# Values on 64 rows, variance and logits side by side, token weights as a row, and the one-hot matrix as eight compares

## The reference

```python
# token selection
scores = einsum('bnd,d->bn', x, w) + b[0]
top_scores, top_indices = top_k(scores, 204)
h = take_along_axis(x, top_indices) * sigmoid(top_scores)[..., None]
# attention: q, k, v = layernorm(h) times Wq.T, Wk.T, Wv.T, plus biases
row_mask = (q[:, :, 0] != 0) & (k[:, :, 0] != 0)
prob = softmax(where(mask, q @ k.T / 8, -1e9)); prob = where(mask, prob, 0)
h = h + (prob @ v) @ Wo.T + bo
# mixture of 8 experts, two of them for a token
xn = layernorm(layernorm(h)) * gamma + beta
logits = xn @ Wr + br
w = softmax(top_k(logits, 2))           # spread over the 8 experts
y = sum over e of (gelu(xn @ W1[e] + b1[e]) @ W2[e] + b2[e]) * w[e]
out = h + y
```

## Time and profile before

| | |
|---|---|
| median of 3 runs | 241.83 us (241.67 to 241.98) |
| profiled execution | 241.94 us |
| its span | 240.1 us |
| mean granted TensorE clock | 0.994 |
| PE busy | 218.4 us, 91% |
| VectorE busy | 165.5 us, 69% |
| GpSimd busy | 149.9 us, 62% |
| ScalarE busy | 140.9 us, 59% |
| chain of waits, share of the span | PE 82%, VectorE 10%, ScalarE 3%, issue 2%, DMA 2% |
| DMA | 25.69 MB, mean 107 GB/s |

### The profile page before, as it was taken

The page is one execution under the profiler, slowest core; times in us unless marked ns, Lnnn a source line. Parts: engine busy times, 40 slices in busy tenths (PEclk is TensorE's granted clock), DMA queues, the critical chain, the costliest instruction groups (busy, mean ns, idle before and its releaser), DMA issues.

```text
span 240.1 us, 5180 instructions
## 1 busy us (share of the span) xinstructions
PE 218.4 (91%) x1612; PEld 122.8 (51%) x1612; DVE 165.5 (69%) x551; ACT 140.9 (59%) x343; POOL 149.9 (62%) x194
## 2 busy tenths in 40 slices
PE   0469699899999999999989999999999999999991
PEld 0345478576767676767534544354443534433420
DVE  3899998979899999765645463855657365483362
ACT  2333857767676767576675455555647556466530
POOL 4398584839895969541427784585755546556662
PEclk9999999999999999999999999999999999999997
DMA  5043831132413231102936706717576492854811
GB/s 147 4 135 116 152 119 53 52 117 77 131 43 122 59 100 40 35 28 61 230 86 152 163 0 158 160 26 179 122 183 145 115 239 65 190 111 120 185 29 35
DMA packets 18340, 25.69 MB, mean 107 GB/s; under 512 B 4746, under 2 KB 15370, under 8 KB 18314
## 3 DMA queue, kind: packets, MB, share of 16 engines
q10 hardware_dynamic: 6112, 13.50, 24.0%
q1 hardware_dynamic: 12138, 11.86, 18.7%
q0 software_dynamic: 64, 0.00, 0.0%
HBM read 23.40 MB, written 1.96 MB: 106 GB/s over the span
## 4 chain that ended last, share of the span: by engine, by line
PE 82%; DVE 10%; ACT 3%; issue 2%; DMA 2%; POOL 0%; ACTq 0%; DVEq 0%; POOLq 0%
PE PD L958 20%; PE PD L973 19%; PE PD L881 5%; PE PD L906 5%; PE PD L893 5%; PE PD L836 4%; PE PD L825 4%; PE PD L918 3%; DVE ahead L1139 3%; PE PD L870 3%; PE PD L923 3%; PE PD L860 2%; PE PD L934 2%; PE PD L983 2%; DMA tok_col<-in_L_tok_b 2%
## 5 line engine op out<-in xcount | busy, mean ns | idle before, releaser
L1280 DVE SCALAR_TENSOR_TENSOR ye<-PD,b_col,mb 128x408 f32<-128x408 f32 x64 | 41.0, 641 | 48.9 <-PE PD L973 48.0
L502 POOL TENSOR_TENSOR acc<-acc,ye 128x408 f32<-128x408 f32 x52 | 54.6, 1050 | 31.8 <-DVE ye L1280 29.1
L675 ACT ACTIVATE hid<-PD,b_eff 128x816 f32<-128x816 f32 x64 | 56.7, 935 | 26.1 <-PE PD L958 25.1
L958 PE MATMUL PD<-uT,w_g 64*128 64x408 f32 x256 | 53.0, 530 | 1.3 <-ACT hid L675 0.9
L973 PE MATMUL PD<-hid,w_sb 128*64 128x408 f32 x256 | 51.1, 519 | 0.2 <-DVE ye L1280 0.2
L634 ACT ACTIVATE E<-PD,nmax 102x204 f32<-102x204 f32 x64 | 26.7, 437 | 15.6 <-DVE nmax L1176 15.6
L958 PEld LDWEIGHTS PD<-uT,w_g 64*128 64x128 f32 x256 | 21.9, 186 | 20.3 <-ACT hid L675 6.7
L973 PEld LDWEIGHTS PD<-hid,w_sb 128*64 128x64 f32 x256 | 15.5, 136 | 32.0 <-issue 26.6
L479 POOL TENSOR_TENSOR rstd<-veps,neg_half 102x8 f32<-102x8 f32 x8 | 13.1, 1640 | 19.2 <-DVE veps L1198 19.2
L1139 DVE SCALAR_TENSOR_TENSOR ahead<-srow,score,PD 128x256 bf16<-128x256 f32 x56 | 23.0, 475 | 0.0
L1176 DVE TENSOR_REDUCE nmax<-PD 102x2 f32<-102x408 f32 x32 | 17.1, 575 | 2.5 <-PE PD L881 1.7
(11 more groups left out here) (169 smaller groups left out, 343.1 us busy)
## 6 DMA issues: line engine op xcount, KB each, us to landing
mb<-mixd ACTq DMA_DIRECT2D x28, 408.0 KB, 5.8
srow<-scored SPq DMA_DIRECT2D x7, 512.0 KB, 4.0
rdbc<-rdend SPq DMA_DIRECT2D x16, 102.0 KB, 2.8
rbc<-rstd2d SPq DMA_DIRECT2D x16, 102.0 KB, 2.9
mb<-mixd SPq DMA_DIRECT2D x4, 408.0 KB, 6.8
X<-in_x ACTq DMA_DIRECT2D x6, 256.0 KB, 3.1
out<-y SPq DMA_DIRECT2D x7, 204.0 KB
w_raw<-in_L_ffn_W SPq DMA_DIRECT2D x2, 256.0 KB, 5.6
```

The source lines that it names most:

```text
L502: pool.tensor_tensor(acc[n % 4][:, :], H[:, n, :] if e == 0 else acc[n % 4][:, :], ye[k % 4][:, :], ALU.add)\
L675: act.activation(hid[k % 4][:, :, :], hid_ps[k % 2][:, :, 0:C], ACT.Gelu, bias=b1_eff[:, e:e + 1]).then_inc(hid_ok, 1)
L958: last = pe.matmul(hid_ps[k % 2][:, p, 0:C], w1_g[halves[p], e, :], uT[halves[p], n, :], start=True, stop=True)
L1280: dve.scalar_tensor_tensor(out=ye[k % 4][:, :], in0=y_ps[k % 2], scalar=b2_col[:, e:e + 1], in1=mb[n % MB][:, e, :], op0=ALU.add, op1=ALU. ...
```

## The change

**Token weights.** `tok_row` is a row on one partition. SyncE loads the weight as its first DMA and ScalarE the bias as its second; GpSimd's two DMAs go. One matmul of one row of ones with that row (L1055) replaces the two transposes. It waits for the DMAs and for VectorE's first memsets, no longer for GpSimd's constants.

**Gate.** `one_plus` (exp(-score) + 1, 128x8) moves from VectorE to ScalarE, right behind the exponential it uses at the start, and behind `copy_denT` in a stage.

**One-hot.** Eight `tensor_scalar` compares of 204 columns, each with a rank per partition from PSUM, replace the `tensor_tensor` of 1632. In stage 0, `copy_v(0)` and `row_max(0,0)` go ahead of `one_hot(1)`.

**Values.** Eight matmuls of 64 rows and 66 moving columns replace four of 128 rows and 132. v's layout follows, in SBUF and in PSUM.

**Variance** of units 0 to 5: `variance2_wide` is four matmuls with 32 weight columns (`ones2`, now 32 wide), each into 32 partitions of its own, behind `values`. ScalarE copies the tile and adds eps (`copy_wide2`). `variance2_rows` is one matmul between `attend(s-1,0)` and `scores(s,1)`, and ScalarE copies the 102x8 result behind `softmax(s,0)`; VectorE's `var_eps2` goes from the stages. Units 6 and 7, in the expert part, keep the old form.

**Logits** in the same way: four matmuls into 32 partitions each, a copy on ScalarE (`copy_logits`), and one transpose (`turn_logits`). The wide part of unit 0 lies ahead of `project(6)`, of unit 1 ahead of `project(7)`, and of unit n ahead of the `hidden` with k % 8 = 4; the transposes lie where `logits` was, but for unit 1, whose transpose moves to the end of stage 7.

**Mix.** One transpose of 102 x 64 in place of four; `copy_mT` is 64 x 102; `write_mix` writes 64 pieces of 408 bytes in place of 16 of 1632.

**Orders.** ScalarE's `copy_std2T(5)` and `gap_tanh(1)` go behind gelu(1). VectorE's `route(1,0)` goes ahead of `copy_ET0(7)`. The next to last store moves from SyncE to ScalarE.

The diff, cut to its core:

```diff
+            sp.dma_start(tok_row[:, 0:D], tok_w.unsqueeze(0)).then_inc(tok_in, 16)
             load_x0(sp, 0)
             load_x(sp, 1)
...
-                sp.dma_start(mixd[n], mT[:, :]).then_inc(mixd_ok, 16)
+                sp.dma_start(mixd[n].rearrange("r (g q) -> g r q", g=G), mT[:, :]).then_inc(mixd_ok, 16)
...
-            pool.dma_start(tok_col[:, 0:1], tok_w.unsqueeze(1)).then_inc(tok_in, 16)
-            pool.dma_start(tok_col[0:1, 1:2], tok_b.unsqueeze(1)).then_inc(tok_in, 16)
...
             load_x0(act, 1)
+            act.dma_start(tok_row[:, D:D + 1], tok_b.unsqueeze(0)).then_inc(tok_in, 16)
...
+            def one_plus_exp(u):
+                act.wait_ge(expneg_ok, u + 1)
+                if u == 0:
+                    act.wait_ge(dve_prep, 2)
+                if u >= 2:
+                    act.wait_ge(spread_ok, SPREAD * (u - 1))
+                    act.wait_ge(gate_ok, u - 1)
+                act.activation(one_plus[u % 2][:, :], expneg[:, :], ACT.Identity, bias=one_col[:, 0:1]).then_inc(plus_ok, 1)
...
+            def copy_wide2(u):
+                act.wait_ge(wide2p_ok, u + 1)
+                if u >= 1:
+                    act.wait_ge(var2p_ok, u)
+                act.activation(wide2[:, :], wide2_ps[u], ACT.Identity, bias=eps_col[:, 0:1]).then_inc(wide2_ok, 1)
+
+            def copy_var2(u):
+                act.wait_ge(var2p_ok, u + 1)
+                if u >= 1:
+                    act.wait_ge(rstd2_ok, u)
+                act.activation(veps2[:, :], var2_ps[u], ACT.Copy).then_inc(veps2_ok, 1)
...
+            def copy_logits(n):
+                if n >= 1:
+                    act.wait_ge(lgp_ok, n)
+                act.activation(lgw[:, :], lgw_ps[n], ACT.Copy).then_inc(lgw_ok, 1)
+
             def gelu(k):
                 e = k % NE
                 act.wait_ge(hidp_ok, k + 1)
+                if e == NE // 2 and k // NE + 2 < UNITS:
+                    copy_logits(k // NE + 2)
...
+                if s >= UNITS - 2:
+                    copy_logits(s - (UNITS - 2))
                 if (u := unit(s, 2)) is not None:
                     squares2(u)
+                    copy_wide2(u)
...
                 softmax(s, 0)
+                if (u := unit(s, 2)) is not None:
+                    copy_var2(u)
                 if (u := unit(s, 1)) is not None and s < UNITS - 1:
                     copy_OT(u)
                 softmax(s, 1)
...
             for k in range(K):
                 gelu(k)
-                if k == 0:
+                if k == 1:
                     copy_std2T(UNITS - 3)
                     gap_tanh(1)
-                if k == 1:
                     copy_denT(UNITS - 1)
                     copy_OT(UNITS - 1)
...
+                if u >= UNITS - 2:
+                    logits(u - (UNITS - 2))
...
-                        last = pe.matmul(v_ps[:, pr, qt * 2 * VX:(qt + 1) * 2 * VX], zT[u % 2][:, cols(pr, qt)],
-                                         wv_bd[:, :, :].rearrange("p a c -> p (a c)"), start=True, stop=True)
+                for i in range(2 * R):
+                    for p in range(2):
+                        last = pe.matmul(v_ps[:, p, i * VX:(i + 1) * VX], zT[u % 2][halves[p], i * Q:(i + 1) * Q],
+                                         wv_x[halves[p], :], start=True, stop=True)
...
+            def variance2_wide(u):
+                pe.wait_ge(sq2_ok, u + 1)
+                for g in range(G):
+                    last = pe.matmul(wide2_ps[u][32 * g:32 * (g + 1), :], ones2[:, :], sq2[:, g * Q:(g + 1) * Q],
+                                     start=True, stop=True)
+                last.then_inc(wide2p_ok, 1)
+
+            def variance2_rows(u):
+                pe.wait_ge(wide2_ok, u + 1)
+                pe.matmul(var2_ps[u], wide2[:, :], ident[:, :].rearrange("k (g x) -> k x g", x=32)[:, 0:2, :],
+                          start=True, stop=True).then_inc(var2p_ok, 1)
...
             def logits(n):
                 pe.wait_ge(u_ok, n + 1)
+                for g in range(G):
+                    pe.matmul(lgw_ps[n][32 * g:32 * (g + 1), :], wr_bd[:, :, :].rearrange("p a e -> p (a e)"),
+                              uT[:, n, g * Q:(g + 1) * Q], start=True, stop=True)
+
+            def turn_logits(n):
+                pe.wait_ge(lgw_ok, n + 1)
                 if n == 0:
                     pe.wait_ge(dve_prep, 8)
                 else:
                     pe.wait_ge(mT_ok, n)
-                for g in range(G):
-                    last = pe.matmul(lg_ps[:, 2 * g:2 * g + 2, :], uT[:, n, g * Q:(g + 1) * Q],
-                                     wr_bd[:, :, :].rearrange("p a e -> p (a e)"), start=True, stop=True)
-                last.then_inc(lgp_ok, 1)
+                pe.transpose(lg_ps, lgw[:, :], ident[:, :]).then_inc(lgp_ok, 1)
 
             def turn_mix(n):
                 pe.wait_ge(top, TOP * (n + 1))
-                for g in range(G):
-                    last = pe.transpose(mT_ps[:, g * Q:(g + 1) * Q],
-                                        mix[:, 2 * g:2 * g + 2, :].rearrange("q a e -> q (a e)"), ident[0:Q, 0:Q])
-                last.then_inc(mTp_ok, 1)
+                pe.transpose(mT_ps, mix[:, :, :].rearrange("q g e -> q (g e)"), ident[0:Q, 0:Q]).then_inc(mTp_ok, 1)
...
+            pe.wait_ge(tok_in, 32)
+            pe.wait_ge(dve_prep, 1)
+            pe.matmul(wb_ps, one_row[:, :], tok_row[:, :], start=True, stop=True).then_inc(wbp_ok, 1)
             pe.wait_ge(pool_prep, 4)
-            pe.wait_ge(tok_in, 32)
-            pe.transpose(wb_ps[:, 0:D], tok_col[:, 0:1].to_broadcast([D, P]), ident[0:D, 0:D])
-            pe.transpose(wb_ps[:, D:D + 1], tok_col[0:1, 1:2].to_broadcast([1, P]), ident[0:1, 0:1]).then_inc(wbp_ok, 1)
...
                 values(s)
+                if (u := unit(s, 2)) is not None:
+                    variance2_wide(u)
...
                 if (u := unit(s, 1)) is not None:
                     attend(u, 0)
+                if (u := unit(s, 2)) is not None:
+                    variance2_rows(u)
...
-                if (u := unit(s, 2)) is not None:
-                    variance2(u)
                 if s == UNITS - 1:
                     attend(s - 1, 1)
+                if s == UNITS - 1:
+                    turn_logits(1)
                 turn_exp(s, 0)
 
             hidden(0)
             turn_exp(UNITS - 1, 1)
-            logits(1)
             attend(UNITS - 1, 0)
             hidden(1)
...
-                gs, n = slice(4 * prs[0], 4 * (prs[-1] + 1)), 4 * len(prs)
-                dve.tensor_tensor(pick[u % 2][:, gs, :], row_no[:, None, :].to_broadcast([P, n, S]),
-                                  rank_ps[u % 2][:, gs, None].to_broadcast([P, n, S]), ALU.is_equal)\
-                    .then_inc(pick_ok, len(prs))
+                for pr in prs:
+                    for g in range(4 * pr, 4 * pr + 4):
+                        last = dve.tensor_scalar(pick[u % 2][:, g, :], row_no[:, :], rank_ps[u % 2][:, g:g + 1], None,
+                                                 ALU.is_equal)
+                    last.then_inc(pick_ok, 1)
...
                     compare(u, 1)
+                    if s == 0:
+                        copy_v(s)
+                        row_max(s, 0)
                     one_hot(u)
...
+            route(1, 0)
             copy_ET0(UNITS - 1)
-            route(1, 0)
```

More of the change, by code:

```diff
@@ L149, in audio_tower_kernel @@
         kT = sb("kT", [P, 2, S])
-        v = [sb(f"v{i}", [Q, 2, R, 2, VX]) for i in range(2)]
+        v = [sb(f"v{i}", [Q, 2, 2, R, VX]) for i in range(2)]
         nmax = [sb(f"nmax{i}", [Q, 2 * R]) for i in range(2)]
@@ L198, in audio_tower_kernel @@
         var2_ps = [PD[3][0:Q, b, C:C + 2 * G] for b in bank2]
+        wide2_ps = [PD[3][:, b, C:C + Q] for b in bank2]
         rstd2T_ps = [PD[3][0:2 * G, b, C:C + Q] for b in bank2]
@@ L210, in scratch @@
             return PD[0][0:Q, 1, i * 64:(i + 1) * 64].rearrange("p (g e) -> p g e", e=NE)
-        lg_ps, sel1_s, lg2_s, both_s, diff_s = (scratch(i) for i in range(5))
+        sel1_s, lg2_s, both_s, diff_s = (scratch(i) for i in range(1, 5))
+        lg_ps = PD[0][0:Q, 1, 344:344 + P]
+        lgw_ps = [PD[1 if n <= 1 else 2][:, 0, C:C + Q] for n in range(UNITS)]
         top1_s, pm1_s, pm2_s = (PD[0][0:Q, 1, 320 + 8 * i:328 + 8 * i] for i in range(3))
-        fall_s = PD[0][0:Q, 1, C:C + NE]
+        fall_s, rden, rden_q = (PD[0][0:Q, 1, 480 + 8 * i:488 + 8 * i] for i in range(3))
         wqT_ps, wkT_ps, woT_ps = PD[3][:, 0, 0:D], PD[3][:, 0, D:2 * D], PD[3][0:D, 0, 2 * D:3 * D]
@@ L717, in _ @@
                     copy_denT(u)
+                if (u := unit(s, -2)) is not None:
+                    one_plus_exp(u)
                 if s == UNITS - 1:
@@ L876, in scores @@
                 pe.wait_ge(k_ok, u + 1)
+                if pr == 0 and u >= UNITS - 2:
+                    pe.wait_ge(lgw_ok, u - (UNITS - 2) + 1)
                 if pr == 1:
@@ L905, in attend @@
                     for p in range(2):
```

(31 more changed lines are left out.)

76 lines of the change are left out of this document (45 added, 31 removed).

## The result

The changed kernel took 251.47 us (median of 4 runs, 250.98 to 252.37) against 241.79 for the kernel before: a ratio of 1.040 (95% interval 1.037 to 1.044). Forecast were 236.2, and 232.8 to 240.0. The profiled execution took 250.98, with a span of 248.6. A few runs of this study were over 1.5% slower than the fastest of their kernel; the medians include them, the ratios leave them out, and the profiles of e2 and e3 are of such runs.

The account below looks back on a forecast made before the run. PE, busy 91% of the span, was taken to bind, with VectorE's work before 30 us. 241.94 -3.5 (start) +1.5 (stages) -0.9 (expert start) -2.7 (expert steps) gave 236.3, as median 236.2; range 232.8 to 240.0.

Parts of the forecast that it names:

- the price of the eight compares: VectorE's one-hot set: taken as 1.85, the present time, between a low of 1.11 and a high of 2.24.
- slack in stages 1 to 6: VectorE's slack of 0.9 behind the pick covers its price; beyond it each 0.1 costs 0.1 a stage.
- a rival with 0.09 and 244.4: Compares wait for GpSimd, 2.1 a stage: 244.4 us, chance 0.09; from 1.85 blocked, (1.85-0.9)x6 = 5.7 eats the gain.
- So no term below counts on the clock: PE was taken to run at its upper level, 2.4 GHz, throughout, so no term included a clock change.
- The variance: Stages 2 to 7: +0.2 for each of six stages from the regrouped PE work, plus 0.33 for logits(0): +1.5.
- The turn that ScalarE binds: Behind attend(s-1,1): PE needs 2.74, ScalarE's 3.07 binds, so only 0.31 of 0.64 is won; period 12.33 against 12.12.
- The values: PE in the stages: eight pass pairs at 0.82 in place of 0.90, so -0.08.
- The start: Earlier bias and lone VectorE multiplication bring the first compare to 8.8; with stage 0's order -3.5.
- the turn that I had named: Turn of stage 0's first exponentials: at 26.5 in place of 30.03.
- The expert part: Expert start -0.9, and expert steps -2.7 from turn_mix (-1.4) and logits (-1.3).
- The column tiles: Wide groups run tiles side by side at 0.33; rival that they don't: +6.8, 243.0 us, chance 0.03.
- The wait ahead of hidden(3): Where the experts begin: a 0.91 wait for a gelu goes when two ScalarE instructions move behind gelu(1): -0.9.

Follow-up runs that it names:

- e2: The kernel before with only the one-hot tensor_tensor replaced by eight tensor_scalar compares of 204: 253.26 us, ratio 1.039.
- e3: The changed kernel with the compares' row numbers on every second word in SBUF: 250.67 us, ratio 1.027.
- e7: e2 with the row numbers read from PSUM, second half repeating the first, so only its times are read: 248.39 us, ratio 1.023.
- e9: The changed kernel with attend(s-1,1)'s four matmuls computed three times more ahead of scores(s,1) in stages 1 and 3: 245.95 us, ratio 1.016.
- e1: The changed kernel with the old one-hot matrix, one tensor_tensor of 1632, in place of the eight compares: 237.76 us, ratio 0.978.
- e5: e1 with the variance of units 0 to 5 in its old form and place, eps added on VectorE: 232.41 us, ratio 0.959.
- e6: e1 with stage 0's old order, copy_v(0) and row_max(0,0) behind the one-hot matrix of unit 1: 236.49 us, ratio 0.976.
- e12: The changed kernel, eight compares kept, with the variance in its old form and place: 242.14 us, ratio 0.999.
- e4: The kernel before with the token weights as a row and nothing else: 239.59 us, ratio 0.987.
- e11: e5 with copy_std2T(5) and gap_tanh(1) between gelu(0) and gelu(1), as before: 233.37 us, ratio 0.963.

## Why the prediction was wrong

**The step that failed** is the one on the price of the eight compares: "I take 1.85", covered by slack in stages 1 to 6. Free, a set costs 2.0 (7x0.240+0.32), so the price was fair. What was wrong is that it depends on GpSimd. I had it as a rival with 0.09 and 244.4, and its mechanism is what happened: one to three compares a stage wait. By the sets' ends, stages 1 and 3 lose 2.6 each, stages 2, 4 and 5 lose 1.1 to 1.7, stage 6 loses 0.8. The mean is 1.7, against the rival's 2.1. I argued against it from the seven old picks of 1855 ns that stood beside the same multiplications without a wait. One of them in the trace of the kernel before:

```profile
45.60 1.04 POOL L473 TENSOR_TENSOR XZ<-X,inv 128x512 f32<-128x512 f32 x1
...
46.15 1.85 DVE L1148 TENSOR_TENSOR pick<-row_no,PD 128x1632 f32<-128x1632 f32 x1
...
46.78 1.04 POOL L444 TENSOR_TENSOR X<-X,gate 128x512 f32<-128x512 f32 x1
```

But those are another form: one of their two tensors lies in SBUF and is read at the single rate. The single rate by itself doesn't spare an instruction: VectorE's `xw`, with both inputs in SBUF, took 1.79 beside GpSimd and 0.69 alone. The row said nothing on a form that isn't in the trace. The lock, which I had cited beside it from the Trainium skill (SBUF — State Buffer, "SBUF: two separate sides"), did bear on it. The slack of 0.9 held about 1 us (e7), as assumed.

**The rival was sized too low** for want of the clock. "So no term below counts on the clock" was true for a PE without holes, and the change tore holes of 2.3 us. That is some 6 us of the 14 lost in the stages (e9 got 5.5 back). By the rival's own rule, which left the clock out, 1.7 blocked per stage would still have left a gain of 0.9: (1.7-0.9)x6 is 4.8, against 5.7. "2.4 GHz, throughout" was not true of the start either: the trace of the kernel before lists its first clock at 18.9 us, and the select_z that began at 15.68 took 3.06, where a later one took 1.60.

**The variance** was forecast at +1.5 and costs 4.0 by the profiles (e1 to e5). The turn that ScalarE binds was right: from the end of the second attend to `turn_exp(3,1)` e6 took 3.09 (forecast 3.07), and its period is 12.3 (forecast 12.33). What was mis-sized is the period without it. I compared with 12.12, a mean over stages of which one holds `logits(0)`; from project(2) to project(5) the stages came every 11.9 before. The values win 0.2 a stage in place of the 0.08 that I took, which makes 11.7. So the new form costs 0.6 a stage: its two groups add 0.75 (e6 against e5, forecast 0.66), and the shorter turn gives back 0.13 in place of 0.31. Its second effect, the shifted alignment of GpSimd and VectorE, was not in the text; it is what is left of e12's 9.3 when the 4 are taken off, one fall of the clock with it.

Two of the sums don't come out, and nothing hangs on it: 6x0.21+0.33 is 1.6 and not 1.5, and the range from its own terms is 233.1 to 239.8.

**What held.** The start: the first compare at 8.18 (forecast 8.8), worth 3.1 by e4's profile, whose median stands 3.3 below its kernel before (forecast 3.5 with the order of stage 0). In the changed kernel only 1.9 of it reached the turn that I had named: that one started at 27.95 on the timeline, against 29.86 before (30.03 on the chain) and 26.5 forecast. Two compares of unit 0 waited for GpSimd as well (967 and 1099 ns), and project(0) came 1.3 later than in e1. In e5, without the compares, the turn started at 25.77. The expert part: -3.8, forecast -3.6. My cut at hidden(0) also takes the 0.65 of `logits(1)` out of the experts, so the like figure of the forecast is -4.2; against it stands a new wait of 0.78 ahead of a `centre2`, for VectorE. Its terms, on the chain of the changed kernel, against the earlier trace rows:

```profile
164.61 0.31 PE PD L995 x8
...
172.03 0.25 PE PD L1004
...
182.05 0.21 PE PD L1008
```

That is 0.56 for the logits (forecast 0.61, before 0.82) and 0.21 for the turn (forecast 0.25). The column tiles do run side by side. The wait ahead of hidden(3) is gone; e11 brings 1.0 us of it back by the medians and 0.6 by the trace up to the next `second` (forecast 0.9). Without the compares the kernel took 237.76, inside the range that the whole change had, but in part by luck: the variance cost 2.5 more than forecast, and the values won more.
